# Linear attention of a two-layer decoder: raw cubed queries produced transposed, two tiles a step, last keys ahead of last queries

## The reference, cut to what matters

```python
q, k, v = qkv[0], qkv[1], qkv[2]                 # of the normalised rows
q = _norm_last(jax.nn.relu(q) + EPS); k = _norm_last(jax.nn.relu(k) + EPS)
q = _norm_last(q ** FOCUS); k = _norm_last(k ** FOCUS)      # FOCUS = 3
kv = jnp.einsum('bhnd,bhne->bhde', k, v)
z = 1.0 / (jnp.einsum('bhnd,bhd->bhn', q, k.sum(axis=2)) + EPS)
out = jnp.einsum('bhnd,bhde,bhn->bhne', q, kv, z)
conv = xp[:, 0:N, :] * w_dwc[:, 0] + xp[:, 1:N + 1, :] * w_dwc[:, 1] + xp[:, 2:N + 2, :] * w_dwc[:, 2] + b_dwc
out = out + conv
return jnp.einsum('bnc,oc->bno', out, w_proj) + b_proj
```

## Time and profile before

| | us |
|---|---|
| median of 3 runs (1680.15 to 1682.77) | 1681.12 |
| span of the profiled execution | 1681.4 |
| expert loop from its first queries to the barrier (1314.9 to 1438.9) | 124.0 |
| `linear_attention` (1438.9 to 1490.3) | 51.4 |

### The profile page before, as it was taken

The page is one execution under the profiler, slowest core; times in us unless marked ns, Lnnn a source line. Parts: engine busy times, 40 slices in busy tenths (PEclk is TensorE's granted clock), DMA queues, the critical chain, the costliest instruction groups (busy, mean ns, idle before and its releaser), DMA issues. The chain is left out here.

```text
span 1681.4 us, 36595 instructions
## 1 busy us (share of the span) xinstructions
PE 1598.4 (95%) x14449; PEld 634.1 (38%) x14452; DVE 1499.6 (89%) x2182; ACT 1319.1 (78%) x2590; POOL 406.3 (24%) x666
## 2 busy tenths in 40 slices
PE   6999999999999999999999999999989999889997
PEld 3542222222223232223322222222235555657774
DVE  6899999989999999989899999999948887688876
ACT  4618999879988989898899999999985565545544
POOL 5800110212223312312211111111013443533302
PEclk9999999999999999999999999999999999999999
DMA  4001001001101200101221011010002000015551
GB/s 147 14 7 20 14 14 14 14 14 22 31 14 21 45 14 14 33 17 27 70 55 26 14 21 20 14 27 14 14 28 63 1 1 1 1 31 95 101 102 51
DMA packets 148026, 52.32 MB, mean 31 GB/s; under 512 B 137424, under 2 KB 146128, under 8 KB 147600
## 3 DMA queue, kind: packets, MB, share of 16 engines
q1 hardware_dynamic: 147152, 48.62, 14.1%
q10 hardware_dynamic: 704, 1.38, 0.2%
HBM read 14.07 MB, written 2.10 MB: 10 GB/s over the span
## 5 line engine op out<-in xcount | busy, mean ns | idle before, releaser
L968 DVE TENSOR_REDUCE mxp<-ps_m 128x2 f32<-128x1024 f32 (+2 forms) x928 | 1049.3, 1198 | 41.3 <-PE ps_m L747 39.9
L897 ACT ACTIVATE work<-ps_s 128x512 f32<-128x512 f32 x1856 | 1001.7, 598 | 76.7 <-PE ps_s L771 48.9
L797 PE MATMUL ps_av<-work,vst 128*32 128x256 f32 x7424 | 592.8, 391 | 14.7 <-ACT avs L904 12.3
L771 PE MATMUL ps_s<-qb,k_stack 50*128 50x512 f16 x1856 | 565.8, 382 | 0.5 <-ACT v_rows L915 0.3
L747 PE MATMUL ps_m<-k_stack,qa 48*128 48x512 f16 (+1 forms) x2048 | 534.1, 358 | 2.3 <-PEq L1123 0.5
L797 PEld LDWEIGHTS ps_av<-work,vst 128*32 128x32 f32 x7424 | 147.0, 108 | 383.2 <-ACT work L897 321.6
L771 PEld LDWEIGHTS ps_s<-qb,k_stack 50*128 50x128 f16 x1856 | 119.7, 94 | 378.6 <-ACT work L897 323.4
L747 PEld LDWEIGHTS ps_m<-k_stack,qa 48*128 48x128 f16 x2048 | 108.2, 93 | 21.5 <-DVE mxp L968 14.8
L616 POOL TENSOR_SCALAR mtmp<-negm 128x16 f32<-128x16 f32 x32 | 8.2, 255 | 390.5 <-DVE negm L973 390.4
L602 POOL COPY vst<-v_rows 128x1024 f32<-128x1024 f32 (+1 forms) x32 | 30.6, 956 | 144.5 <-PE ps_av L797 144.5
L682 POOL TENSOR_TENSOR q_rows<-avs,rc 128x256 f32<-128x256 f32 x31 | 19.2, 619 | 173.3 <-DVE rc L979 173.3
(11 more groups left out here) (441 smaller groups left out, 2006.1 us busy)
## 6 DMA issues: line engine op xcount, KB each, us to landing
x_res<-in_x SPq DMA_DIRECT2D x4, 512.0 KB, 8.2
w_experts<-in_w_experts SPq DMA_DIRECT2D x1, 2048.0 KB, 8.0
out<-x_res SPq DMA_DIRECT2D x8, 256.0 KB, 2.2
v_rows<-in_ctx_c SPq DMA_DIRECT2D x1, 1664.0 KB, 7.3
work<-in_ctx_t SPq DMA_DIRECT2D x1, 1456.0 KB, 15.8
ctx_n<-in_ctx_n SPq DMA_DIRECT2D x1, 1248.0 KB, 8.0
w_qkv<-in_w_qkv ACTq DMA_DIRECT2D x1, 768.0 KB, 8.6
w_qkv<-in_w_qkv SPq DMA_DIRECT2D x1, 768.0 KB, 4.2
```

The costliest lines, as they stand in the source:

```text
L771: pe.matmul(ps_s[:, bank, :], STACKS[part(n)][rows, group(n) * PAIRS + j, t * P:t * P + P], qb[n % 2][rows, :, j, :], start=True, stop=Tru ...
L797: m = pe.matmul(ps_av[32 * h:32 * h + 32, cols], vst[n % 2][:, t, h, :], pbuf[(tau[n] + t) % 2][:, h, cols], start=(t == 0 and half == 0), ...
L897: a.activation(pbuf[g % 2][:, h, :], ps_s[:, b, :], ACT.Exp, scale=factor).then_inc(s["exp"], 1)
L968: v.tensor_reduce(dst, src, AX.X, ALU.max).then_inc(s["mred"], 1)
```

## The change

In `projection_experts_queries` the queries aren't normalised any more, and they come out of TensorE with channels on partitions: `turned_queries` puts the weights where the rows were, four products of 128 columns in place of a 256-column half of two. GpSimd cubes them (`query_cubes`) and stores them in `qf`; VectorE cubes, sums and inverts only the 256 key columns. GpSimd also adds the projection's bias there (`plus`), behind each tile. For the last tile the keys are made first, and its queries behind its values (`last_queries`, `relu_last`, `squared_last`). The norm of tiles 12 to 14 has its front half behind step 15's mixture and its back half in step 16; the norm of tile 15 goes from step 17 to steps 16 and 17. The cast of the context rows is cut into four, at the ends of steps 17 to 20. The eight idle products are gone.

In `linear_attention` there is no turning or copying of queries. A step takes a couple of tiles: eight numerator products into two banks, one reciprocal of 32 columns straight from PSUM, one multiplication of 512 columns, four transposes, one copy. Denominator and numerator columns are interleaved, 17 to a head, and the epsilon is in the key sums. `add` takes 512 columns. The scaling of `fold` and the copy of `side` go from VectorE to ScalarE, `wide` and a memset to GpSimd, and the order is written out call by call. Couples are numbered 0 to 7.

```diff
-    FOCUSED_NORMS = ((0, 4, 5), (4, 8, 9), (8, 12, 13), (12, 15, 15), (15, 16, 17))
+    FOCUSED_NORMS = ((0, 4, 5), (4, 8, 9), (8, 12, 13), (12, 15, 15), (15, 16, 16))
+            def query_cubes(f):
+                if f < T - 1:
+                    g.wait_ge(s["sq"], f + 1)
...
+                g.tensor_tensor(qf[:, f, :], square[f % 2][:, 0:D], fa[f % 2][:, 0:D], ALU.mult).then_inc(s["q"], 1)
+
+            def plus(f):
+                g.wait_ge(s["xf"], f + 1)
+                g.tensor_tensor(x[:, f, :], x[:, f, :], after[:, :], ALU.add).then_inc(s["plus"], 1)
...
-                    share(f, 1, k_ring[f % RING][:, :], s["k"])
-                    share(f, 0, qf[:, f, :], s["q"])
+                if f == T - 1:
+                    plus(f)
+                    key_shares(f)
+                    query_cubes(f)
+                elif f is not None:
+                    query_cubes(f)
+                    key_shares(f)
...
+                if f < T - 1:
+                    turned_queries(c, query_bank(c))
                 for k in range(2):
-                    m = pe.matmul(query_bank(c)[:, :], xo[c % 2][:, 2 + k, :], w[:, k, 0:2 * D], start=(k == 0), stop=(k == 1))
+                    m = pe.matmul(query_bank(c)[:, D:2 * D], xo[c % 2][:, 2 + k, :], w[:, k, D:2 * D], start=(k == 0), stop=(k == 1))
...
+            def turned_queries(c, out):
+                for j in range(2):
+                    for k in range(2):
+                        m = pe.matmul(out[:, j * P:j * P + P], w[:, k, j * P:j * P + P], xo[c % 2][:, 2 + k, :],
+                                      start=(k == 0), stop=(k == 1))
...
-                if n == T + LAG:
-                    pe.wait_ge(s["gused"], T)
-                    idle_products(pe, logit[:, :], weh[:, 0, 0:P], weh[:, 0, 0:512], 8)
+                if f == T - 1:
+                    last_queries(f, c)
...
-                v.tensor_tensor(cube[f % 2][:, :, :], square[f % 2][:, :, :], fa[f % 2][:, :, :], ALU.mult).then_inc(s["cube"], 1)
+                    v.wait_ge(s["k"], f - 1)
+                v.tensor_tensor(cube[f % 2][:, :, :], heads(square[f % 2][:, D:2 * D]), heads(fa[f % 2][:, D:2 * D]), ALU.mult)\
+                 .then_inc(s["cube"], 1)
```

Of `linear_attention` these lines carry the prediction:

```diff
+            def numerators(p):
+                if p >= 2:
+                    pe.wait_ge(s["o"], p - 1)
+                for t in range(2):
                     for j in range(2):
+                        m = pe.matmul(ps_n[:, p % 2, t, j * N:j * N + N], qt[:, 2 * p + t, j * P:j * P + P],
+                                      bd[:, j, :, :].rearrange("p h c -> p (h c)"), start=True, stop=True)
...
+            def shares(p):
+                r = p % 2
+                v.wait_ge(s["num"], p + 1)
+                v.reciprocal(rz[r][:, :, :], shared(r)[:, :, :, HD]).then_inc(s["rz"], 1)
...
+                v.tensor_tensor(o[r][:, :, :].rearrange("p t (g d) -> p t g d", d=HD), shared(r)[:, :, :, 0:HD],
+                                rz[r][:, :, :].unsqueeze(3).to_broadcast([P, 2, 2 * NH, HD]), ALU.mult).then_inc(s["o"], 1)
...
+            def add(q):
+                rows = x[:, 2 * q:2 * q + 2, :]
+                v.wait_ge(s["prod"], q + 1)
+                v.tensor_tensor(rows, prod[:, q % 2, :].rearrange("p (t d) -> p t d", t=2), rows, ALU.add).then_inc(s["x"], 1)
+                v.wait_ge(s["x"], q + 1)
+                for n in (2 * q, 2 * q + 1):
+                    m = v.bn_stats(st[:, n, :], x[:, n, :])
+                m.then_inc(s["st"], 1)
```

More of the change, by code:

```diff
@@ L1557, in _ @@
                     biased(n + LEAD + 1)
+                if f is not None and f < T - 1:
+                    plus(f)
             g.wait_ge(s["q"], T)
+            g.wait_ge(s["plus"], T)
         @block.tensor
@@ new lines, in _ @@
+            pe.wait_ge(s["set"], 5)
+            numerators(0)
+            numerators(1)
+            folded_bias()
+            turn(0)
+            numerators(2)
+            turn(1)
+            numerators(3)
+            turned_peaks()
+            turn(2)
+            numerators(4)
+            spread_peaks()
+            turn(3)
+            numerators(5)
+            turn(4)
+            numerators(6)
+            turn(5)
+            numerators(7)
+            turn(6)
+            project(0)
@@ L2125, in _ @@
+            turn(7)
+            project(1)
+            project(2)
+            project(3)
+            turn_first()
+            project(4)
+            query_first()
+            project(5)
+            project(6)
+            project(7)
         @block.scalar
         def _(a):
-            def turned(n):
-                a.wait_ge(s["tq"], n + 1)
-                if n >= 2:
-                    a.wait_ge(s["num"], n - 1)
-                a.copy(qt[n % 2][:, :, :], ps_q[n % 2][:, :, 0:P]).then_inc(s["qt"], 1)
@@ new lines, in ahead, with window_early @@
+                a.activation(lt[:, j, 0:c1 - c0], ot[:, j, c0:c1], ACT.Copy, scale=tap[:, j, 0:1]).then_inc(s["lt"], 1)
+            def window_early(i):
+                for j in range(2):
+                    middle(i, j)
+                    ahead(i, j)
+            a.wait_ge(s["pad"], 1)
+            out(0)
+            a.wait_ge(s["fold"], 3)
+            a.activation(side[:, 0:D + 1], ps_c[:, 0:D + 1], ACT.Copy, scale=1.0 / 16.0).then_inc(s["side"], 1)
+            out(1)
+            a.wait_ge(s["tap1"], 1)
@@ new lines, in _ @@
+            window_early(0)
+            out(2)
+            out(3)
+            window_early(1)
+            a.wait_ge(s["fold"], SCALED)
+            a.activation(fold[:, :, :], ps_f, ACT.Copy, scale=part[:, 0:1]).then_inc(s["scaled"], 1)
+            out(4)
+            out(5)
+            window_early(2)
+            out(6)
+            middle(3, 0)
+            middle(3, 1)
+            out(7)
+            middle(4, 0)
+            middle(4, 1)
+            a.wait_ge(s["var"], 1)
+            a.activation(tmp[:, 0, 0:FIRST_T], tmp[:, 1, 0:FIRST_T], ACT.Sqrt).then_inc(s["root"], 1)
@@ L2177, in _ @@
+            a.wait_ge(s["xtr"], 1)
+            a.copy(xt[:, :, :], first_x[:, 0:2, :]).then_inc(s["xcp"], 1)
+            a.wait_ge(s["qm"], 1)
+            for c in range(2):
+                a.activation(qh[:, c, :], first_x[:, 2 + c, :], ACT.Identity, bias=near[:, c:c + 1]).then_inc(s["qh"], 1)
             a.wait_ge(s["qh"], 2)
@@ new lines, in left, with right @@
+            def left(i, j):
+                c0, c1 = columns(i)
+                v.wait_ge(s["mid"], 2 * (i - LATE) + j + 1)
+                v.scalar_tensor_tensor(yt[:, j, c0:c1], ot[:, j, c0:c1], tap[:, j, 0:1], yt[:, j, c0:c1],
+                                       ALU.mult, ALU.add).then_inc(s["late"], 1)
+            def right(i, j):
+                c0, c1 = columns(i)
+                v.wait_ge(s["ot"], reach(i))
+                if i < LATE:
+                    v.wait_ge(s["left"], 2 * i + j + 1)
+                else:
+                    v.wait_ge(s["late"], 2 * (i - LATE) + j + 1)
@@ new lines, in _ @@
+            v.tensor_scalar(tap1[:, :], tap[:, :, 1], 1.0, None, ALU.add).then_inc(s["tap1"], 1)
+            peaks_of_weights()
+            shares(0)
+            shares(1)
+            peak_of_bias()
+            shares(2)
+            peaks_over_rows()
+            shares(3)
+            shares(4)
+            scales()
+            shares(5)
+            right(0, 0)
+            right(0, 1)
+            shares(6)
+            shares(7)
+            add(0)
+            right(1, 0)
+            right(1, 1)
@@ L2316, in _ @@
+            add(1)
+            norm_front()
+            right(2, 0)
+            right(2, 1)
+            add(2)
+            norm_back()
+            left(3, 0)
+            left(3, 1)
+            v.wait_ge(s["pad"], 1)
+            right(3, 0)
+            right(3, 1)
+            add(3)
+            left(4, 0)
+            left(4, 1)
+            right(4, 0)
+            right(4, 1)
+            add(4)
+            add(5)
+            first_low()
+            add(6)
+            add(7)
             v.wait_ge(s["ql"], 2)
-            v.wait_ge(s["st"], T)
```

425 lines of the change are left out of this document (178 added, 247 removed).

## The result

| | before | after |
|---|---|---|
| median, us (4 runs each) | 1680.78 (1680.15 to 1682.77) | 1663.77 (1663.42 to 1665.12) |
| span of the profiled execution | 1681.4 | 1662.0 |
| step 6's queries to the barrier's end | 124.2 | 115.9 |
| barrier's end to the next stage's first row | 51.5 | 41.6 |

The ratio is 0.9899, 95% interval 0.9887 to 0.9911: 17.0 us less, where 17.3 were forecast. The spans of the two profiled executions differ by 19.4, of which 1.3 us arise in the last 23 us of arithmetic, which the change doesn't touch: the mean granted clock was 0.85 there before and 1.00 after.

A forecast was written before the change was run, and what follows sets the result against it. Waits, not full engines, were taken as what could be won in the expert loop with its tail and in `linear_attention`: -7.6, -10.2 and +0.5 for the next stage sum to -17.3, giving 1664 us, range 1659 to 1672.

The forecast's parts named there:

- Loop: Expert loop, steps 6 to 14: VectorE's shorter cube chain leaves TensorE late next; -2.2 us, bounds -2.7 and -0.8.
- Step 15: Step 15 of the expert loop: its norm no longer stands ahead of tile 10's rows; -1.4 us.
- Tail: Tile 10's to tile 15's queries: 20.25 us become 18.1, with waits of 0.45 and 0.8; -2.1 us.
- Last tile: Tile 15, first product to last `outer`: keys first, queries behind, 6.57 us shortened; -1.9 us.
- VectorE's work in `linear_attention`: VectorE's listed instructions in `linear_attention`, from opening to first norm and its low part, sum to 33.2 us.
- Waits: VectorE's waits in `linear_attention`: 4.9 us in all, including 2.25 for bias products and 1.45 ahead of the first add.
- The clock: `linear_attention`'s weight product and first records run at 1.2 GHz behind the barrier; +1.6 us, from 0 to 3.
- The port: `linear_attention`: GpSimd's left parts slow VectorE's right taps, two hits; +1.0 us, 0 to 2.6.
- Next stage: Entry of `cross_one_head`: TensorE ends its projections early and may enter colder; +0.5 us, 0 to 1.5.
- Rival (a): Loop and `linear_attention`: GpSimd holds VectorE's port, loop gains only 0.8, left parts cost 2.6; 1667 us, chance 0.17.
- Rival (b): `linear_attention` and tail: waits only move, six later couples each wait 1 us, tail waits stay; 1673 us, chance 0.13.
- Rival (d): `linear_attention`: TensorE stays at 1.2 GHz, its 31 us take 62; 1684 us, slower; chance 0.04.

The follow-up runs named there:

- norms_back: Changed kernel with the two expert-loop norms back in steps 15 and 17; 1667.50 us, ratio 0.9907 to the kernel before.
- hold_left: Changed kernel with GpSimd's left parts of the second window held until VectorE has applied the first right taps; 1661.92 us, ratio 0.9873 to the kernel before.
- idle_inside: Changed kernel with eleven unread f32 products on TensorE ahead of turn 6 in `linear_attention`; 1663.68 us, ratio 0.9883 to the kernel before.
- idle_restored: Changed kernel with the eight removed idle products put back ahead of the last `outer` product; 1663.38 us, ratio 0.9886 to the kernel before.
- idle_end: Changed kernel with seven unread f32 products behind TensorE's last projection of `linear_attention`; 1665.79 us, ratio 0.9897 to the kernel before.
- last_undone: Changed kernel with tile 15 treated as the other tiles; 1666.87 us (median of three of four executions), ratio 0.9903 to the kernel before.
- project_first: Changed kernel with couple 0's projection ahead of couple 6's turn on TensorE; 1662.30 us, ratio 0.9874 to the kernel before.

## Why the prediction was right, and where its terms were not

The total, -17.3, came out at -17.0 by the medians and -17.8 by the three stretches of the trace (-8.3 to the end of the barrier, -9.9 in `linear_attention`, +0.5 in the next stage). The mechanism held in both stages, but that the numbers agree so well is in part luck: the loop gave 1.5 more than forecast, the tail, the last tile and the barrier's pause took back 0.9, and the low clock cost what was forecast at another place. Term by term:

- **Loop, -2.2: measured -3.7** (85.0 us for 88.7). The mechanism held: the chain over VectorE went under TensorE's list. The price of the 128-column queries was read from a row of eight records as 0.97, and here they take 0.89, so TensorE's list is 9.04 and not 9.15. The five steps without a projection fell to that list, from 48.0 to 45.2 us, -2.8; at the forecast's 9.2 to 9.3 each it would have been -1.5 to -2.0. The four with a projection gained 0.9 together, where the forecast left them 0.2 to 0.7. The bound of -2.7 was too narrow for this.
- **Step 15, -1.4: -1.6.** norms_back shows the cause.
- **Tail, -2.1: -1.9**, waits of 0.27 and 1.24 for the forecast 0.45 and 0.8. The mis-sized term is the chain to tile 15's rows: it is put at 4.5 us (its parts add up to 4.25) and took 5.2 from the queries' end at 1407.30 to the turn at 1412.48, since the front half of the norm, "0.65", took 1.5 beside GpSimd (1410.22 to 1411.70). A tile took 3.29 and not 3.37, which gives 0.4 back. "I take none" for products at the low clock was right, without a reason given, and matters more than I saw (1.5 us, norms_back).
- **Last tile, -1.9: -1.5.** The mis-sized term is "2.9" for the keys' chain: it took 3.5 (1424.80 to 1428.32), 0.4 of the difference in VectorE's cube, which took 0.83 beside GpSimd's bias addition. The barrier's pause, which the sum doesn't have, grew by 0.29 besides (1.48 for 1.19).
- **VectorE's work in `linear_attention`, 33.2: 32.8** (41.3 from its first to its last row, less 6.5 of waits and the port's 1.94). **Waits, 4.9: 6.5.** The 2.25 for the bias products came as 1.06 and 1.21. All of the difference lies in "1.45 ahead of the first add": it measured 3.11. But with TensorE at the full clock it measured 1.49 (hold_left, idle_inside, idle_restored), so the wait was sized rightly, and the 1.6 on top of it are the low clock of the next point.
- **The clock, +1.6 at the weight product: 0 there**, in the profiled execution, and 1.7 in six others. In its place 1.6 us of low clock stood at turn 6, a pause I had seen as a wait and not as a clock. The sum was right for the wrong place, by luck: idle_end, norms_back and last_undone have both costs, 5.34 us in the opening and 18.3 to 18.6 in the middle.
- **The port, +1.0: +1.94**, one hit of two instructions. I took two hits of single taps. Outside `linear_attention`, where the forecast has no term for it, 0.86 of the tail's chain (much as before the change) and 0.4 of the last tile's are its doing.
- **Next stage, +0.5: +0.5.** Of it 0.2 to 0.3 is the clock; the cause of the rest is open.

Rival (a) is refuted in its main place: VectorE's cube starts first and takes 0.42 in each of the steps 6 to 14, and the queries are 9.04 apart. Its second half, left parts against right taps at up to 2.6, is where 1.94 lies. Rival (b), the waits only move: VectorE's waits in the stage sum to 6.5 us and not over 9, and of the six later couples one waits for its numerators, 1.21 us, behind the bias products. Rival (d): mean clock 0.96 in the stage, far from its condition. Of "cheaper than I think" (c) nothing came in sum.

## What to carry to other kernels

When a change moves work to GpSimd, look at which VectorE instruction starts beside it and who is first: the later one waits whole instructions. When a wait on TensorE is priced, price the clock of what follows too: pauses of 2.05, 2.31 and 2.66 us here cost another 1.5 or 1.6. And check whether an instruction that others wait for stands behind one that isn't ready yet: the swap of a projection and a turn gave 3.0 us with two lines, 1.4 by the order and 1.6 by the clock.

## What the runs showed of the hardware

- Pauses of TensorE of 0.73, 1.24 and 1.66 us (the last in project_first), and one of 1.81 us in `linear_attention` (ahead of L2165), were followed by the full clock in every trace that has them. One of 1.48 us at the barrier (1.39 in last_undone) was followed by 1.2 GHz in six executions of ten; 0.7 us of products separate it from another pause of 1.16 us (2.03 in last_undone), and where idle products fill that one, 1.23 us at the barrier was followed by the full clock in both executions. So the length of a single pause doesn't decide. One of 2.22 us ahead of the next stage was followed by 1.2 GHz in seven of nine, one of 2.65 us in six of seven, and those of 2.05 us (the kernel before) and 2.31 us (norms_back) in their one execution. Four records of 256 columns (f32) then take 1.71 us (1422.00 in the kernel before) in place of 0.87.
- Instructions on one column pay the port too: two norm instructions of 0.16 us took 0.60 and 0.58 beside GpSimd (1410.42 and 1411.12), each up to the end of the GpSimd instruction that had started first.
- Two right taps took 1.40 alone, 3.34 beside two GpSimd additions and 2.45 or 1.67 beside the end of them; the two additions took 2.59 alone and 2.95 there. VectorE's shares, which read PSUM and one SBUF tile, took 0.69 with GpSimd running beside them (1447.77 in hold_left) as without.
